# Preamble arithmetic handed from VectorE to GpSimd, and a planner that spaces count groups by TensorE's work alone

## The reference, cut to what matters

```
x = x + _L0_gnn_ref(_layernorm(x), relvectors, w_ih, w_hh, b_ih, b_hh, src, dst, edge_type_16)
    msg = h[edge_src] + relvectors[edge_rel]
    red = jax.ops.segment_sum(msg, edge_dst, num_segments=h.shape[0])
    return _gru_cell(red, h, w_ih, w_hh, b_ih, b_hh)
x = x + _L0_ffn_ref(_layernorm(x)[None], Wg, bg, W1, b1, W2, b2)[0]      # top 2 of 8 experts
```

## Time and profile before

| | before |
|---|---|
| median of 3 runs | 1611.08 us (1608.55 to 1616.82) |
| the profiled execution | 1608.13 us |
| its span in the trace | 1606.3 us, mean granted TensorE clock 0.909 |
| busy: TensorE, VectorE, ScalarE, GpSimd | 1333.8, 1100.4, 708.4, 1034.2 us |

### The profile page before, as it was taken

How to read it: one execution, slowest core, us unless ns; L and a number is a source line. 1 busy time by engine, 2 the same in 40 slices (tenths; PEclk the granted TensorE clock), 3 DMA queues, 4 the chain that set the end, 5 groups by cost and what they waited for, 6 DMA issues and landing times. The chain is left out here.

```text
span 1606.3 us, 37371 instructions
## 1 busy us (share of the span) xinstructions
PE 1333.8 (83%) x12905; PEld 1025.3 (64%) x12905; DVE 1100.4 (69%) x3994; ACT 708.4 (44%) x1538; POOL 1034.2 (64%) x948
## 2 busy tenths in 40 slices
PE   1269999999989999989889998784653899999991
PEld 1235656666656666666667766564653799999991
DVE  7867677577777777778979888953545455555550
ACT  6334444444445554434433332221221676667660
POOL 2177777566777777676777777777773255555552
PEclk9959999999999999999998999686766899999996
DMA  9676544344554455444544544446652455555556
GB/s 304 175 214 197 153 127 114 109 132 133 138 146 137 132 148 143 123 115 142 145 132 146 146 133 112 113 120 211 236 119 60 100 101 94 95 94 96 94 80 179
DMA packets 136158, 220.43 MB, mean 137 GB/s; under 512 B 27761, under 2 KB 101046, under 8 KB 134688
## 3 DMA queue, kind: packets, MB, share of 16 engines
q0 software_dynamic: 63872, 123.12, 31.7%
q1 hardware_dynamic: 72096, 94.84, 19.7%
HBM read 169.05 MB, written 57.76 MB: 141 GB/s over the span
## 5 line engine op out<-in xcount | busy, mean ns | idle before, releaser
L667 POOL DMA_INDIRECT ring<-h_table,idx x728 | 727.2, 999 | 316.2 <-issue 254.8
L780 ACT ACTIVATE amat<-P 128x300 f16<-128x300 f32 (+3 forms) x608 | 230.6, 427 | 398.0 <-PE P L1642 396.2
L1655 PE MATMUL P<-hs,amat 128*126 128x512 f16 (+4 forms) x1323 | 356.9, 399 | 0.0
L721 POOL DMA_INDIRECT out_rows<-yo,xrows x112 | 176.5, 1576 | 162.4 <-DVE yo L1527 114.6
L1140 DVE TENSOR_SCALAR cone<-iota,comb 128x294 f16<-128x294 f16 (+3 forms) x840 | 258.2, 310 | 0.0
L1139 DVE TENSOR_SCALAR lone<-iota,slo 128x128 f16<-128x128 f16 x840 | 223.7, 267 | 15.7 <-PE P L1637 15.2
L1637 PE MATMUL P<-cone,lone 128*128 128x294 f16 (+3 forms) x840 | 164.6, 291 | 52.3 <-ACT amat L780 32.5
L1655 PEld LDWEIGHTS P<-hs,amat 128*126 128x126 f16 (+4 forms) x1323 | 160.7, 137 | 71.9 <-issue 8.2
L1518 DVE SCALAR_TENSOR_TENSOR gl<-gT,scales,gh 128x512 f16<-128x512 f32 x112 | 84.2, 752 | 126.1 <-ACT gh L904 126.1
L1869 PE MATMUL P<-xh,w_all 128*128 128x256 f16 x896 | 157.0, 274 | 0.0
L676 POOL DMA_INDIRECT expert_rows<-xrow,slots x100 | 121.6, 1216 | 54.3 <-issue 26.8
(11 more groups left out here) (240 smaller groups left out, 2666.3 us busy)
## 6 DMA issues: line engine op xcount, KB each, us to landing
raw<-in_L_ffn_W_dram SPq DMA_DIRECT2D x32, 512.0 KB
xrows<-expert_rows SPq DMA_DIRECT2D x56, 257.0 KB, 3.2
ring<-h_table,idx POOLq DMA_INDIRECT x728
w_parts<-parts SPq DMA_DIRECT2D x16, 512.0 KB
w_all<-w_parts SPq DMA_DIRECT2D x8, 1024.0 KB
h_in<-h_table SPq DMA_DIRECT2D x25, 250.0 KB
x<-in_x_dram SPq DMA_DIRECT2D x25, 250.0 KB
out_rows<-x SPq DMA_DIRECT2D x25, 250.0 KB
```

What stands on the lines that cost most here:

```text
L667: nc.gpsimd.indirect_dma_start(out=ring[:, r, j, :], out_offset=None, in_=h_dram, in_offset=bass.IndirectOffsetOnAxis(ap=idx[:, slot, g * ...
L721: nc.gpsimd.indirect_dma_start(out=out_dram, out_offset=bass.IndirectOffsetOnAxis(ap=xrows[:, b % XR, j, D:D + 1].bitcast(I32), axis=0), i ...
L780: nc.scalar.activation(amat[:, b % 2, :, s * aw:(s + 1) * aw], P[2 + g % 2][:, 0:HIS * aw].rearrange("p (h w) -> p h w", w=aw), ACT.Copy). ...
L1655: nc.tensor.matmul(both, amat[:, b % 2, hi, 0:used], hs[:, hi, :], start=(hi == 0), stop=False)
```

## The change

Two things.

1. **Preamble work on GpSimd.** `rest(0)`, `rest(2)` and `rest(4)`, the split of the relation vectors (six instructions at the start of `small_weights`), and two of the three instructions that begin `head_keys` are issued by GpSimd. VectorE keeps the bit mask `slo_i`, now ahead of `bases()`, and waits for the keys (`s_keys`) at the start of `small_weights`. SyncE waits on `s_rest2` for chunks 0, 2 and 4.
2. **The planner's cost** of a count group is k * 0.22 + 0.09 * aw in place of k * 0.5 + 0.09 * aw. No instruction is added or taken away by this; groups, pieces and some tiles move between half steps.

```diff
+POOL_RESTS = (0, 2, 4)
...
-    cost = np.cumsum([k * 0.5 + 0.09 * aw for _, _, k, aw in GROUPED])
+    cost = np.cumsum([k * 0.22 + 0.09 * aw for _, _, k, aw in GROUPED])
...
             for c in range(LN_CH + 1):
-                sp.wait_ge(s_rest1, c + 1)
+                if c in POOL_RESTS:
+                    sp.wait_ge(s_rest2, POOL_RESTS.index(c) + 1)
+                else:
+                    sp.wait_ge(s_rest1, c + 1 - sum(n < c for n in POOL_RESTS))
...
+            def rest(c):
+                pool.wait_ge(s_part1, c + 1)
+                at = hs[:, c * LN_J:c * LN_J + LN_J, :]
+                nc.gpsimd.tensor_tensor(at[:, :, D:PD], xc[:, c % XB, :, :], at[:, :, 0:D], ALU.subtract).then_inc(s_rest2, 1)
+
+            rest(0)
+            rest(2)
+            pool.wait_ge(s_rel, 16)
+            pool_link(nc.gpsimd.tensor_scalar(rel_rest, rel_raw, UP, None, ALU.mult))
+            for part in range(PARTS):
+                pool_link(nc.gpsimd.tensor_copy(rels[:, part, :], rel_rest))
+                if part + 1 < PARTS:
+                    pool_link(nc.gpsimd.tensor_tensor(rel_rest, rel_rest, rels[:, part, :], ALU.subtract))
+            rest(4)
+            pool.wait_ge(s_keys, 1)
+            nc.gpsimd.tensor_copy(slo[:, :], slo_i[:, :])
+            pool_link(nc.gpsimd.tensor_copy(comb[:, :], src_t[:, 0:HEAD * GC]))
+            nc.gpsimd.tensor_tensor(comb[:, :], comb[:, :], slo[:, :], ALU.subtract).then_inc(s_keys, 1)
...
             def small_weights():
-                dve.wait_ge(s_rel, 16)
-                link(nc.vector.tensor_scalar(rel_rest, rel_raw, UP, None, ALU.mult))
-                for part in range(PARTS):
-                    link(nc.vector.tensor_copy(rels[:, part, :], rel_rest))
-                    if part + 1 < PARTS:
-                        link(nc.vector.tensor_tensor(rel_rest, rel_rest, rels[:, part, :], ALU.subtract))
+                dve.wait_ge(s_keys, 2)
...
             coefficients(2)
-            rest(0)
             edge_windows()
             rest(1)
             coefficients(3)
             statistics(4)
-            rest(2)
...
-            rest(4)
             rest(5)
             rest(6)
+            dve.wait_ge(s_tr_out, RT)
+            nc.vector.tensor_scalar(slo_i[:, :], src_t[:, 0:HEAD * GC], 127, None, ALU.bitwise_and).then_inc(s_keys, 1)
             bases()
...
             def head_keys():
-                n = HEAD * GC
-                link(nc.vector.tensor_scalar(slo_i[:, :], src_t[:, 0:n], 127, None, ALU.bitwise_and))
-                nc.vector.tensor_copy(slo[:, :], slo_i[:, :])
-                link(nc.vector.tensor_tensor(comb[:, :], src_t[:, 0:n], slo_i[:, :], ALU.subtract))
```

More of the change, by code:

```diff
@@ L451, in gnn_ffn_kernel @@
         names = """
-            s_const s_ones s_pads s_wnat s_weights s_rel s_ln_var s_ln_std s_ln_coef s_ln_h s_part1 s_rest1 s_natf
+            s_const s_ones s_pads s_wnat s_weights s_rel s_ln_var s_ln_std s_ln_coef s_ln_h s_part1 s_rest1 s_rest2 s_keys s_natf
             s_viol s_violb s_natd s_base s_based s_tr s_dst_out s_tr_out s_flag s_bias s_zero s_small s_init
@@ L463, in gnn_ffn_kernel @@
             tx_done xh_ready xl_ready w1_ready l1_done gelu_done g_high g_low l2_done y_out firsts_ready
-            out_written dve_chain late_chain
+            out_written dve_chain late_chain pool_chain
         """.split()
-        (s_const, s_ones, s_pads, s_wnat, s_weights, s_rel, s_ln_var, s_ln_std, s_ln_coef, s_ln_h, s_part1, s_rest1, s_natf,
+        (s_const, s_ones, s_pads, s_wnat, s_weights, s_rel, s_ln_var, s_ln_std, s_ln_coef, s_ln_h, s_part1, s_rest1, s_rest2, s_keys, s_natf,
          s_viol, s_violb, s_natd, s_base, s_based, s_tr, s_dst_out, s_tr_out, s_flag, s_bias, s_zero, s_small, s_init,
@@ L477, in gnn_ffn_kernel @@
          tx_done, xh_ready, xl_ready, w1_ready, l1_done, gelu_done, g_high, g_low, l2_done, y_out, firsts_ready,
-         out_written, dve_chain, late_chain) = [sem(n) for n in names]
+         out_written, dve_chain, late_chain, pool_chain) = [sem(n) for n in names]
         s_nat = [sem(f"s_nat{n}") for n in range(3)]
@@ L659, in _, with pool_link @@
                 nc.gpsimd.tensor_copy(nat[:, c + 1, :, :], nat_i[:, c + 1, :, :]).then_inc(s_natf, 1)
+            made = [0]
+            def pool_link(ins):
+                made[0] += 1
+                ins.then_inc(pool_chain, 1)
+                pool.wait_ge(pool_chain, made[0])
+            def rest(c):
[15 more added lines that the diff above has]
+            nc.gpsimd.tensor_tensor(comb[:, :], comb[:, :], slo[:, :], ALU.subtract).then_inc(s_keys, 1)
             pool.wait_ge(s_tr, 3 * RT + 6)
```

## The result

The changed kernel takes 1632.06 us in the median of 4 runs (1624.95 to 1638.47), the kernel before 1611.08 beside it, in the median of its three fast runs (a fourth, slow one took 1812 us and is left out): ratio 1.0124, 95% interval 1.0100 to 1.0147, slower by 20 us (16 to 24). The forecast was +11.2 us. The profiled execution takes 1624.95 us, its span 1623.0 at a granted clock of 0.905, so the two traces differ by 16.7 us.

A forecast was written before the change was run, and what follows sets the result against it. TensorE was taken to bound steps 9 to 68, VectorE to lead steps 69 to 76, and GpSimd's transfers to bound steps 1 to 8. Preamble +5.7 and loop +5.5 made +11.2 us on 1611.1: 1622.3 us, range 1606 to 1634.

The forecast's parts named there:

- both parts costing: Whole kernel: the main forecast that preamble and loop changes both cost, 1622 us (1619.5 to 1632), chance 0.50.
- code load: Preamble, ahead of GpSimd's first subtraction: fetching the instruction's code from HBM takes one landing, 7.9 us (bounds 0 and 15.8).
- the loop's +5.5 us: Loop, from the planner's cost: -1.5, -16, +9 and +14 us over steps 1 to 76 sum to +5.5.
- rival B: One part costs, the other is a wash: cheap ISA instruction (1616) or late work half absorbed (1614); chance 0.29.
- The subtraction's 3.8 us: Preamble, rest(0) on GpSimd: two passes over 2048 columns, one per input, 3.8 us (bounds 1.89 and 5.7).
- GpSimd also blocks VectorE: Preamble: rest(4) on GpSimd beside first_targets could cost VectorE a whole subtraction, +3.8 us; chance 0.10.
- rival D: Preamble: GpSimd's rest(4) excludes VectorE's first_targets, +3.8 us, 1626 us; chance 0.10.
- VectorE's 4.1 us saved, counted as 0: Start of the loop: relation and key work off VectorE gains nothing, as TensorE's sum waits for a gather (up to 3.8).
- The preamble's sum: Preamble: ScalarE 6.1 us late on chunk 4, less 0.4 gained by bases(), makes +5.7 us (bounds -0.4 and +15.5).
- upper bound of 10.7: Steps 49 to 68: 9 chunks and 40 pieces more cost TensorE at most +10.7 us; +9 counted, lower bound +3.
- 13 to 26 us idle: Late stages: both engines have this much idle time, given as support for one part being a wash.
- Rival C: Late steps: idle time takes nearly all added work, loop -13 us, 1597.7 us with a cheap ISA instruction; chance 0.11.

The follow-up runs named there:

- e4: The kernel before with only the relation split and keys moved to GpSimd, three rests on VectorE, cost k * 0.5: 1617.29 us, ratio 1.0037.
- e3: The kernel before with only the three rests of chunks 0, 2 and 4 moved to GpSimd, cost k * 0.5: 1610.67 us, ratio 1.0001.
- e15: The kernel before with only rest(2) moved to GpSimd, cost k * 0.5, on a slower chip: 2007.62 us against 2001.72, ratio 1.0008.
- e9: e2 with one wait more, so that GpSimd begins the keys only after VectorE finishes bases(): 1616.42 us against 1610.19 for the kernel before, ratio 1.0022.
- e2: The changed kernel with the planner's cost put back to k * 0.5, so only the preamble differs from before: 1619.04 us, ratio 1.0041.
- e1: The kernel before with only the planner's cost changed to k * 0.22, preamble untouched: 1624.32 us against 1611.27, ratio 1.0078.
- e17: Third run of the kernel before with only the planner's cost changed to k * 0.22: 1624.45 us against 1613.33, ratio 1.0079.

## Why the prediction was right and wrong

The direction, both parts costing, and the range (1606 to 1634) held; the size, 20 us against 11.2, did not. Two steps of the sum failed. The preamble was charged 7.9 us for a code load that took no time and nothing for GpSimd holding up VectorE, which moved the loop's start by some 9 us. And the loop's +5.5 us measured +12.6, of which the stages show 8.6 and the rest has no place.

**The code load: wrong.** The step "I take one landing, 7.9 us" measured 0.06 us; rival B's first condition, a cheap ISA instruction, was the right one. The subtraction's 3.8 us measured 4.05. With these two, the forecast's own sum for the preamble would have been -0.4. Chunk 4's statistics began at 34.04 and not at 42.

**"GpSimd also blocks VectorE", held as rival D at 0.10 and put at nothing in the sum: right, at three places and not one.** The wait of ScalarE behind `nmr`, 2.4; behind `tmin`, 5.20 where it was 1.37, 3.8; in `bases()` 0.85 + 0.79 + 1.81 less three times 0.17, 2.9. They add up to 9.1, and the loop starts 9.7 us later. Part of that match is chance: the first two make 6.2, but `bases()` begin 5.5 late (62.64 for 57.12); behind the third `bases()` end 8.5 late, the first gather goes out 9.2 late, TensorE's first sum begins 7.4 late and the first addition 9.7. Rival D had the second place, `rest(4)` beside `first_targets`, and its size (+3.8); it missed the other two, whose victims are of 4 to 16 columns. It was luck that the forecast named about 63 for `bases()`: they began at 62.64, for another reason. The rule weighed there from the Trainium skill (SBUF — State Buffer, Who interferes with whom) says that a GpSimd instruction that reads SBUF and a VectorE one with two SBUF inputs, or in a two-port mode, exclude each other for a whole instruction, and that whoever issues first wins. The traces agree on the order, since in `e4` GpSimd is the one that waits, and on the two inputs, which `nmr` (held in `e3` and `e15`) and the rows of `bases()` have; the batch statistics (2.71 us) are unhurt. `var` and `tmin` have one input and are held all the same, so by the rule they would have to run in a two-port mode. For `tmin` a row of the kernel before fits that (its 512 columns take 0.42 us, those of the two-input instruction behind it 0.69); for `var` no row shows its mode. That `e9` puts the three rows back by time alone makes the hold-up shown and not argued.

**VectorE's 4.1 us saved, counted as 0:** right, and for the reason given. TensorE's wait for `group_f` did shrink, from 8.95 to 5.62 us, but its first sum of gathered rows then waited for its gather, and from the end of `bases()` to the first addition it is 26.7 us where it was 25.4.

**The preamble's sum:** +5.7 forecast, +6.6 (3.4 to 9.7) measured; that is luck, as two errors cancelled. By the trace alone it would be +9.5. That some 3 us of a late start are not in the time is seen in `e2`: 98.43 + 83.2 for steps 1 to 8 is 181.6 where before has 175.15, so 6.4 of the 9.5 are left.

**The loop: the term that was mis-sized.** +5.5 forecast, +12.6 measured twice. By stages, mean of three profiled executions with k * 0.22 (after, `e1`, `e17`) against five with k * 0.5 (before, `e2`, `e3`, `e4`, `e9`):

| steps | forecast | k * 0.5 | k * 0.22 | difference |
|---|---|---|---|---|
| 1 to 8 | -1.5 | 84.0 | 82.3 | -1.7 |
| 9 to 48 | -16 | 520.0 (514.6 to 528.3) | 501.3 | -18.7 |
| 49 to 68 | +9 | 256.5 | 269.2 | +12.7 |
| 69 to 76 | +14 | 104.2 | 118.8 | +14.6 |
| 77 to 90 | 0 | 153.6 | 155.2 | +1.6 |

Steps 49 to 68 cost more than their upper bound of 10.7. The prediction called them TensorE's (231.3 us busy) and read its idle 25.9 us as room. GpSimd was fuller: 194.4 us busy and 53.1 of issue in 257.2, and it was named as the bound of steps 1 to 8 only. But it doesn't set the pace behind the change. Its groups in steps 49 to 68, of the kernel before and of the changed one:

```profile
L667 POOL DMA_INDIRECT ring<-h_table,idx x165 | 165.5, 1003 | 54.0 <-issue 47.3 <-PE P L1590 6.4 <-DVE idx L1072 0.3
```

```profile
L697 POOL DMA_INDIRECT ring<-h_table,idx x162 | 162.4, 1003 | 64.5 <-issue 46.0 <-PE P L1610 17.8 <-DVE idx L1096 0.6
```

GpSimd's busy and issue time, with that of its other transfers, is 247.5 us before and 248.6 after, and its wait for TensorE's sums grew by 11.4 us. TensorE's added work was paid in full: its idle time was no room. That this is because the engines take turns, TensorE in some steps and GpSimd in others, is argued; no run separates the steps.

In steps 69 to 76 the work on VectorE was put too small: the prediction had 20 chunks, 6.8 us, in steps 73 to 76, the window has 28 chunks more (`lone` and `cone` builds x156 for x128), and VectorE is busy 13.8 us more, though the stage's sum came out right. In steps 1 to 8 the order lists of step 3 shown ahead of the prediction have 5 chunks and 24 pieces each, so they don't show fewer; the table of the plan does. The stage took 81.3 us in the changed kernel, under the 86.4 that the prediction gave GpSimd's transfers: 63 of them lie in its window and not 67. Two of the prediction's side sums are off as well: "13 to 26 us idle" for both engines leaves out VectorE's 40.5 us in steps 49 to 68, and late work taken up by half would make B's loop -1.5 - 16 + 11.5 = -6 and not -3.

The table sums to +8.6, and the expert phase adds -0.2 (402.3 and 402.1). The other 4 us are in no stage that can be shown: only profiled executions can be split, and those with k * 0.22 lay 3.5 us under their kernels' medians on average (-7.1, -3.5, 0.0), those with k * 0.5 1.4 above (-3.0, +4.0, +0.7, +6.3, -0.9). This closes the sum (8.4 + 3.5 + 1.4 = 13.3) but names no place; it stays open. Steps 9 to 48 alone scatter by 13.7 us over the five traces with k * 0.5, which puts their mean out by some 2.6 us (an estimate, the standard error), so the 4 us can also be scatter.

**Rival C, late idle absorbs, and rival B:** neither; at 0.22 steps 49 to 90 cost 29 us together, and at 0.8 steps 49 to 76 gave back 4.5.

No version with the real counts beat the kernel before: `e3` and `e15` are level with it, and both directions of the cost and the one tried of `FREE_FROM` lose.

## What to carry to other kernels

Before moving work to GpSimd, list what VectorE issues while it runs, the tiny instructions first: one of eight columns took 4 us here, and who is hit changes when the start moves by 2 us (`e15`). Put such work where VectorE has statistics to take (2.71 us with and without it), or behind the chain, as `e9` does; one input alone is no protection, as `var` and `tmin` show. And before spreading work by one engine's cost, add up each engine's busy and issue time by stage: in steps 69 to 76 GpSimd stood at 97.6 of 104.1 us, so work taken away gave back 1.6 us, while work added cost 14.6.

## What was not expected of the hardware

A wait of TensorE of a few us can come with a lower granted clock behind it. These are 10 us windows from 210 us, of the kernel before and of `e4`, whose loops are the same instructions, 0.9 us apart at the end of the first stage:

```profile
210.00:220.00 10.00, 9.00 (x122) 5.80 (x122) 9.45 (x43) 5.71 (x14) 6.38 (x7) 1.00 0.36 107
220.00:230.00 10.00, 10.00 (x56) 5.99 (x55) 7.64 (x35) 3.21 (x8) 7.50 (x9) 1.00 0.44 128
```

```profile
210.00:220.00 10.00, 6.98 (x69) 4.38 (x70) 9.59 (x37) 3.70 (x9) 5.02 (x5) 0.62 0.29 82
220.00:230.00 10.00, 10.00 (x85) 5.93 (x84) 6.70 (x31) 3.24 (x10) 5.88 (x7) 0.86 0.47 130
```

TensorE waited 3.0 of 10 us, and the mean granted clock was 0.62 (between the levels of 1.2 and 2.4 GHz) and still 0.86 in the fully busy window behind. Steps 9 to 48 of one and the same plan took 514.6 to 528.3 us, the later stages with it scattered by 1.6 to 3.3 us. A single trace of this kernel tells its longest stage to some 7 us, which is as much as the terms at stake.
